# Feed-forward weights quantised inside the last two attention units, and a weight stage that only transposes

## The reference, cut to what matters

```python
h = _layernorm(x) * (1 + ca) + sa
x = x + ga * _L0_attn_ref(h, W_qkv, W_out)            # 16 heads, causal, ALiBi
h = _layernorm(x) * (1 + cb) + sb
x = x + gb * _L0_ffn_ref(h, w_gate, w_up, w_down)     # 704 x 256, 704 x 256, 256 x 704
...
def fp4_quant_dequant(x):        # along the last dim, blocks of 16
    scale = max(abs(xb)) / 6, at least 1e-12
    return nearest of (0, .5, 1, 1.5, 2, 3, 4, 6) to abs(xb / scale), * sign * scale
def _L0_ffn_ref(x, w_gate, w_up, w_down):
    gate, y = q(x) @ q(w_gate).T, q(x) @ q(w_up).T
    return q(silu(gate) * y) @ q(w_down).T
```

## Time and profile before

| | |
|---|---|
| median of 3 runs | 4037.24 us (4034.93 to 4038.52) |
| profiled execution | 4047.3 us, its span 4045.3 us |
| TensorE, VectorE, ScalarE, GpSimd busy over the span | 85%, 85%, 61%, 63% |
| attend's own work | 262 to 1245 us |
| last unit with row maxima | ends 1192 us |
| first instruction of prepare | 1249.56 us |
| first DMA of feed_forward | 1303.87 us |

### The profile page before, as it was taken

The page is one execution under the profiler, slowest core; times in us unless marked ns, Lnnn a source line. Parts: engine busy times, 40 slices in busy tenths (PEclk is TensorE's granted clock), DMA queues, the critical chain, the costliest instruction groups (busy, mean ns, idle before and its releaser), DMA issues. The chain is left out here.

```text
span 4045.3 us, 64173 instructions
## 1 busy us (share of the span) xinstructions
PE 3418.7 (85%) x22940; PEld 1634.9 (40%) x22940; DVE 3430.8 (85%) x5768; ACT 2465.4 (61%) x4542; POOL 2561.4 (63%) x2392
## 2 busy tenths in 40 slices
PE   5979999999994899999777888888888788777667
PEld 2633333333332555555433333333333333333366
DVE  5768888888863999999669999999999999999866
ACT  5626666666773344444477777777777777676422
POOL 1102232322331888888578999989989999888633
PEclk8979999999997999999898989888988999898689
DMA  4894656555532111111122332332233322322232
GB/s 137 282 198 64 88 72 90 78 82 83 82 47 73 38 49 45 46 45 40 34 75 61 88 89 80 83 83 74 76 82 86 86 78 77 87 71 72 57 101 82
DMA packets 291354, 329.66 MB, mean 81 GB/s; under 512 B 37375, under 2 KB 207478, under 8 KB 291030
## 3 DMA queue, kind: packets, MB, share of 16 engines
q1 hardware_dynamic: 291038, 325.58, 35.2%
HBM read 239.58 MB, written 85.03 MB: 80 GB/s over the span
## 5 line engine op out<-in xcount | busy, mean ns | idle before, releaser
L1898 POOL TENSOR_TENSOR d_dBu<-d_dtu,d_Bn 128x1024 f32<-128x1024 f32 x384 | 903.5, 2388 | 19.8 <-DVE d_dtu L2079 19.7
L752 ACT ACTIVATE b_P<-b_pT 128x512 f32<-128x512 f32 (+1 forms) x1120 | 571.7, 575 | 298.2 <-PE b_pT L658 295.2
L1678 ACT ACTIVATE d_dA<-d_dt,d_decay 128x512 f32<-128x512 f32 x768 | 524.4, 685 | 254.4 <-DVE d_h L2006 252.2
L785 DVE CUSTOM_DVE_ANT_0 b_pS<-b_pS,mask_qk 128x512 f32<-128x512 f32 (+1 forms) x768 | 501.7, 690 | 83.6 <-PE b_pS L668 74.2
L1886 POOL TENSOR_TENSOR d_h<-d_h,d_Cn 128x2048 f32<-128x2048 f32 x112 | 511.5, 4574 | 77.9 <-ACT d_last_h L1702 42.4
L630 POOL TENSOR_SCALAR_AFFINE_SELECT b_P<-b_P 128x128 f32<-128x128 f32 (+2 forms) x608 | 194.0, 323 | 513.6 <-ACT b_P L752 501.8
L2006 DVE TENSOR_TENSOR_SCAN d_h<-d_dA,d_last_h,d_dBu 128x512 f32<-128x512 f32 x384 | 462.1, 1263 | 47.3 <-PE d_y L1543 28.7
L668 PE MATMUL b_pS<-KS,QS 99*128 99x512 bf16 (+3 forms) x1536 | 475.1, 339 | 28.3 <-PEq L85 21.5
L2006 DVE TENSOR_TENSOR_SCAN d_h<-d_dA,d_dBu 128x512 f32<-128x512 f32 x384 | 443.2, 1207 | 52.8 <-PE d_y L1543 25.2
L658 PE MATMUL b_pT<-QS,KS 118*128 118x512 bf16 (+3 forms) x1536 | 449.3, 329 | 3.1 <-ACT b_P L752 2.1
L1543 PE MATMUL d_y<-d_h,d_eye 32*32 32x512 f32 x8192 | 345.4, 704 | 32.8 <-DVE d_h L2013 32.8
(11 more groups left out here) (352 smaller groups left out, 6735.3 us busy)
## 6 DMA issues: line engine op xcount, KB each, us to landing
d_Bn<-scratch_bs SPq DMA_DIRECT2D x128, 512.0 KB, 5.0
d_Cn<-scratch_bs SPq DMA_DIRECT2D x112, 256.0 KB, 3.4
scratch_parts<-a_part SPq DMA_DIRECT2D x48, 512.0 KB, 4.1
QS<-scratch_parts SPq DMA_DIRECT2D x192, 128.0 KB, 7.2
KS<-scratch_parts SPq DMA_DIRECT2D x192, 128.0 KB, 7.6
scratch_v<-a_v SPq DMA_DIRECT2D x16, 1024.0 KB, 7.6
V<-scratch_v SPq DMA_DIRECT2D x32, 512.0 KB, 11.6
a_x<-in_L_attn_x_dram SPq DMA_DIRECT2D x16, 512.0 KB, 7.7
```

Of the source, the lines that this page charges most:

```text
L752: act.activation(t[:, heads[0]:heads[-1] + 1, c * CH:c * CH + w], pT[:, place % RING, 0:len(heads) * w].rearrange("p (h w) -> p h w", w=w) ...
L785: last = dve.tensor_tensor_reduce(out=pS[:, j % RING, 0:w], in0=pS[:, j % RING, 0:w], in1=K["mask_qk"][:, 0:w], scale=-1.0, scalar=-MASKED ...
L1678: act.activation(to[:, m % 2, :], dt[:, c.k % 2, m, :], ACT.Exp, scale=decay[:, m, n:n + 1]).then_inc(dA_d, 1)
L1898: pool.tensor_tensor(product(c, n)[:, 2 * j:2 * j + 2, :], dtu[:, c.k % 2, 2 * j:2 * j + 2, :], Bn[:, n // BG % 2, n % BG, :].unsqueeze(1) ...
```

## The change

The tiles of the weights (`raw_gate`, `raw_up`, `raw_down`, `raw_wout`, and `raw_late`, which is the quantising scratch first and takes W_in, W_x and W_dt after it) are now allocated around `attend` and `prepare`, on the other side of SBUF. SyncE issues the five feed-forward loads and the eight of W_out in attention's step u = 8. VectorE clears the pad rows at attention's start, quantises gate and the first half of up after `normalise` of unit 29 (in unit 30's step), and the rest after `normalise` of unit 30 (in unit 31's step). SyncE then loads W_in, W_x and W_dt into the scratch, before the last store. `prepare` loads only base_W, the A and B matrices and a bias (11 DMAs and one), turns gate, up and down first, and copies every second piece out with VectorE.

```diff
+            def load_weights():
+                sp.wait_ge(pads, 2)
+                for w, name in ((gate, "L0_ffn_w_gate"), (up, "L0_ffn_w_up")):
+                    sp.dma_start(w[:, 0:KF - 1, :], A[name][0:(KF - 1) * P, :].rearrange("(r p) k -> p r k", p=P)).then_inc(ffn_in, 16)
+                    sp.dma_start(w[0:FR, KF - 1, :], A[name][(KF - 1) * P:FF, :]).then_inc(ffn_in, 16)
+                sp.dma_start(down[:, :, :], A["L0_ffn_w_down"].rearrange("(r p) k -> p r k", p=P)).then_inc(ffn_in, 16)
+                for r in range(KD):
+                    for i in range(NQB):
...
+            def load_late():
+
+                sp.wait_ge(q_done, 3)
...
             def step(m, u):
+                if u is not None and u.base * NG + u.k == 8:
+                    load_weights()
                 if m is not None and (not isinstance(m.base, int) or m.base * NG + m.k + 1 < total):
...
             units(sp, step)
+            load_late()
             store(LAST)
...
+            dve.memset(gate[FR:P, KF - 1, :], 0.0).then_inc(pads, 1)
+            dve.memset(up[FR:P, KF - 1, :], 0.0).then_inc(pads, 1)
...
+            def quantise_in_drain(u):
+
+                n = u.base * NG + u.k
+                if n == total - 2:
+                    dve.wait_ge(ffn_in, 16 * 5)
+                    block_scales(gate, KF * D)
+                    round_blocks(gate, KF * D)
+                    dve.wait_ge(q_done, 1)
+                    block_scales(up, KF * D)
+                if n == total - 1:
+                    round_blocks(up, KF * D)
+                    dve.wait_ge(q_done, 2)
+                    block_scales(down, KD * FF)
+                    round_blocks(down, KD * FF)
...
+                if u is not None:
+                    quantise_in_drain(u)
             units(dve, step)
...
         @block.tensor
         def _(pe):
-            pe.wait_ge(turn_in, 16 * (14 + KD * NQB))
             for j, (src, dst) in enumerate(turns):
-                if j == early:
-                    pe.wait_ge(q_done, 3)
+                if j == late:
+                    pe.wait_ge(late_in, 16 * (3 + KD * NQB))
+                if j == last:
+                    pe.wait_ge(turn_in, 16 * 11)
                 if j >= 8:
-                    pe.wait_ge(ev, j - 7)
+                    pe.wait_ge(ev if j % 2 == 0 else ev_dve, (j - 8) // 2 + 1)
...
         @block.vector
         def _(dve):
...
+            for j, (src, dst) in enumerate(turns):
+                if j % 2:
+                    dve.wait_ge(tr, j + 1)
+                    dve.tensor_copy(dst, turned(j)).then_inc(ev_dve, 1)
```

More of the change, by code:

```diff
@@ L476, in bank_pieces, with blocks, spread, late_weights @@
     return pieces
+DN, NS, DR, TAPS = 512, 16, 64, 4
+MD = DN // P
+QB = 32
+NQB = P // QB
+FB = 16
+FF = 704
+KF = -(-FF // P)
+FR = FF - (KF - 1) * P
+ROUND = 1.5 * 2.0 ** 22
+DOWN = 1.0 - 2.0 ** -23
+EXPONENT = 0x7F800000
+def blocks(t):
+    return t.rearrange("p (b e) -> p b e", e=FB)
+def spread(s, n):
+    return s.unsqueeze(2).to_broadcast([s.shape[0], n // FB, FB])
+def late_weights(late):
+    w_in = late[:, 0:8 * D].rearrange("p (r k) -> p r k", k=D)
+    w_x = late[0:DR + 2 * NS, 8 * D:8 * D + DN]
+    w_dt = late[:, 8 * D + DN:8 * D + DN + 4 * DR].rearrange("p (r k) -> p r k", k=DR)
+    return w_in, w_x, w_dt
 def attend(nc, A, S, K):
@@ L526, in attend @@
         sems += s_in + [alp_put]
+        ffn_in, late_in = S["ffn_in"], S["late_in"]
+        pads, q_step, q_done = sem("pads"), sem("q_step"), sem("q_done")
+        gate, up, down, late = K["raw_gate"], K["raw_up"], K["raw_down"], K["raw_late"]
+        W = KF * D
+        v, e = late[:, 0:W], late[:, W:2 * W]
+        amax, scale, inv = K["raw_amax"], K["raw_scale"], K["raw_inv"]
         s_mm, s_max, g_tr, g_ev, g_step, g_joined, gc_set, g_parts = (
@@ L834, in sem @@
             return sems[-1]
[L836 to L838 removed]
+        gate, up, down, w_out = K["raw_gate"], K["raw_up"], K["raw_down"], K["raw_wout"]
+        w_in, w_x, w_dt = late_weights(K["raw_late"])
+        base, acat = sb("base", [P, KD, D]), sb("acat", [118, D])
         bcat = sb("bcat", [P, KD, 7, 16])
[L840 to L842 removed]
         psT = [local.enter_context(nc.psum_tensor(f"w_psT{i}", [P, 512], F32)) for i in range(8)]
[L844 removed]
+        turn_in, tr, ev, ev_dve, bias_in = (sem(n) for n in ("turn_in", "tr", "ev", "ev_dve", "bias_in"))
+        late_in = S["late_in"]
+        sems += [S["ffn_in"], late_in]
         turns = []
+        for n, w in enumerate((gate, up)):
+            for r in range(KF):
+                rows = P if r < KF - 1 else FR
+                for k in range(KD):
+                    turns.append((w[0:rows, r, k * P:(k + 1) * P], K["guT"][:, k, n * FF + r * P:n * FF + r * P + rows]))
+        for r in range(KD):
+            for k in range(KF):
+                cols = P if k < KF - 1 else FR
+                turns.append((down[:, r, k * P:k * P + cols], K["downT"][0:cols, k, r * P:(r + 1) * P]))
+        late = len(turns)
         for r in range(8):
@@ L861, in prepare @@
                 turns.append((w_out[:, r, k * P:(k + 1) * P], K["w_outT"][:, k, r * P:(r + 1) * P]))
+        last = len(turns)
+        for r in range(KD):
             for k in range(KD):
@@ L867, in prepare, with turned @@
             turns.append((bcat[:, r, :, :].rearrange("p e r -> p (e r)"), K["bcatT"][0:112, r * P:(r + 1) * P]))
[L868 to L877, removed]
-        block = local.enter_context(nc.Block())
+        block = local.enter_context(nc.Block())
+        def turned(j):
+            src, dst = turns[j]
+            rows, cols = src.shape
+            t = psT[j % 8][0:cols, 0:rows]
+            return t.rearrange("p (i q) -> p i q", q=QB) if len(dst.shape) == 3 else t
         @block.sync
         def _(sp):
[L882 to L893, removed]
             sp.dma_start(base[:, :, :], A["L1_ffn_base_W"].rearrange("(r p) k -> p r k", p=P)).then_inc(turn_in, 16)
@@ L1269 @@
 NATURAL_SET = 6
-QB = 32
-NQB = P // QB
 PE_B = (5, 8, 11, 14)
@@ L2381, in build @@
             prepare(nc, A, S, K)
+            raw.close()
             feed_forward(nc, A, S, K)
```

85 lines of the change are left out of this document (36 added, 49 removed).

## The result

The changed kernel takes 4006.8 us (median of 4 runs, 4004.87 to 4008.9) against 4037.88 us for the kernel before on the same chip (4 runs): ratio 0.9924, 95% interval 0.9907 to 0.9941. The forecast was 4007.6. The profiled execution went from 4047.3 to 4008.9 us, its span from 4045.3 to 4006.8.

The account below looks back on a forecast made before the run. `prepare`, running alone between attention and feed-forward (load, VectorE's quantising, turns), was taken as the bound. 39.7 us gained less 10.0 of collision and 0.1 of clears gives 29.6: 4037.2 to 4007.6, forecast 4003 to 4012 (56%), range 3996 to 4018.

Parts of the forecast that it names:

- The load and the quantising leave `prepare`: At the seam, 9.7 us of load and 35.8 us of quantising go; feed_forward starts 39.7 us earlier.
- the term of the turns: In `prepare`, 76 turns in one row, 21 slow in 4.9 us and 55 in 8.0 us: together 13.3 us.
- The collision: In attention's last two units, GpSimd's selects and VectorE's blocking quantising instructions wait for each other: 10 us lost.
- The walk: Tile-by-tile estimate of select waits in units 30 and 31: 4.2 us and about 6 us.
- no collision: Rival for attention's last two units: selects and quantising run side by side, gain 38.6 us, time 3998.6; 23%.
- a heavy one: Rival: 16 selects in the last units each wait one mean blocking instruction, 18.4 us, time 4016.0; 15%.
- VectorE doesn't bound the drain: VectorE ends at about 1245, before unit 31's invert; the rival, VectorE bounding the drain and a slower kernel, had 2%.
- Late weights: In `prepare`, they land near 1252, before the 37th turn needs them; rival that turns wait, 4010 to 4020, 2%.
- SyncE's queue: Before unit 11's load, thirteen added DMAs take 12.5 us, covered by 21.3 us of idle queue: no cost.
- The sum: Whole kernel: 39.7 - 10.0 - 0.1 = 29.6 us less, profiled execution 4017.7, median 4007.6.

Follow-up runs that it names:

- Experiment 3: Changed kernel with the quantising back at the start of `prepare`, loads early and turns shared as in the change: 4030.3 us, ratio 0.9974.
- experiments 1: Changed kernel with VectorE's 30 quantising instructions left out, so weights stay unquantised: 3997.9 us, ratio 0.9894.
- 8: Changed kernel without quantising; VectorE does eight reductions in the step of attention's last unit instead: 4001.0 us, ratio 0.9897.
- 9: Changed kernel without quantising; VectorE does eight products of two SBUF tiles in the step of attention's last unit instead: 4008.1 us, ratio 0.9915.
- experiments 5: Changed kernel with the quantising's product scratch in PSUM and the late weights issued behind the last store: 4002.4 us, ratio 0.9901.
- 7: Changed kernel with scratch in PSUM, late weights behind the last store, and gate's first four quantising instructions moved before unit 29's invert: 4000.1 us, ratio 0.9894.
- experiment 2: Changed kernel with the quantising's product scratch in PSUM, late weights still before the last store: 4011.9 us, ratio 0.9922.
- 6: Changed kernel with each large quantising product and element-wise instruction cut into three of at most 512 columns: 4003.7 us, ratio 0.9903.
- 10: Changed kernel with the large quantising instructions cut in three and the late weights issued behind the last store: 4002.9 us, ratio 0.9902.
- experiment 4: Changed kernel with all 76 turned pieces copied out by ScalarE alone: 4010.0 us, ratio 0.9923.

## Why the prediction was right

**The load and the quantising leave `prepare`.** Forecast: 39.7 us from `prepare`, feed_forward's first DMA at 1264.2 if attention ended as before. Measured: the stretch from the first instruction of `prepare` to that DMA went from 54.3 us to 11.96 (1257.99 to 1269.95), 42.3 us less. The mechanism is as forecast; the term of the turns was too large, 13.3 us for what took 10.9 (1258.04 to the last copy's end, 1268.9). Most of it is the price of a turn at the fast clock, forecast at 0.145 us "between 0.09 and 0.17": some 17 turns lie in the slow 3.9 us (forecast 21 in 4.9), and the other 59 end at 1268.58, so 6.7 / 59 = 0.113 us each. Over all runs the slow part was 3.6 to 9.0 us, and from first turn to c_wo it took 11.8 to 14.3 us with the copies shared (forecast 14.4): this trace is at the short end. Experiment 3 divides the gain.

**The collision.** Forecast 10 us, 4.2 in unit 30 and about 6 in unit 31; measured 3.1 and 5.4, 8.5 in sum. (The walk's own parts for unit 31 are 4.0, 1.5 and 1, which make 6.5, and 10.7 in all.) The walk said which tiles: 1 (+2.0, measured 1.29), 2 (+1.5, 1.12) and 4 (+0.7, 0.71) in unit 30, and tile 1 of unit 31 as the worst (+4.0, measured 3.00). Tiles 2 and 3 of unit 31, forecast at 2.5 us together, cost about 0.4. What brought the unit near its forecast all the same is a part that the walk didn't contain: TensorE's clock fell to 0.50 during the wait, which cost some 2.0 us. So for unit 31 the mechanism was right and the size was in part luck. That no collision or a heavy one would come instead is excluded by the selects (5.57 us for four) and by experiments 1, 8 and 9. The walk also counted the element-wise and the small instructions as blocking. For the element-wise ones the change's own trace shows it, in the step of unit 31:

```profile
1237.69 0.89 DVE L860 TENSOR_SCALAR raw_late<-raw_late 128x1408 f32<-128x1408 f32 x1
```

```profile
1238.15 0.70 POOL L689 TENSOR_SCALAR_AFFINE_SELECT b_P<-b_P 128x256 f32<-128x256 f32 x1 [1.24 <-ACT b_P L811]
```

The select takes 0.70 us and not 0.41, and ends 0.27 us after the end of L860 (1238.58). The small ones are at least held up themselves: 0.30 us beside selects in unit 30 (L851 and L853 on up), 0.21 alone. That a select waits for a small one is not shown.

The rule of the Trainium skill (SBUF — State Buffer, Who interferes with whom) says this of products and reductions: products of two SBUF inputs block a GpSimd that reads SBUF, reductions don't. Experiments 8 and 9 agree with it, 22.53 against 28.61 us for one unit.

**VectorE doesn't bound the drain.** It was done at 1244.00, forecast about 1245, and 7.80 us before the last inversion. **Late weights.** Issued from 1244.03 on, 8.9 us ahead of the store as forecast (9), and TensorE shows no wait for them. **SyncE's queue.** Forecast 12.5 us for the thirteen DMAs under 21.3 us of idle queue. It was 17.8 us:

```profile
523.94 0.58 SPq L633 DMA_DIRECT2D raw_gate<-in_L_ffn_w_gate_dram  x1
524.56 3.88 SPq L634 DMA_DIRECT2D raw_gate<-in_L_ffn_w_gate_dram  x1
...
529.50 1.52 SPq L634 DMA_DIRECT2D raw_up<-in_L_ffn_w_up_dram  x1
...
531.71 10.04 SPq L639 DMA_DIRECT2D raw_wout<-in_L_attn_W_out_dram  x8
544.99 0.34 SPq L240 DMA_DIRECT2D QS<-scratch_parts  x1
```

The queue held the second DMA of gate for 3.88 us, where 0.55 was put in. The load of unit 11 still starts at 544.99, as before at 545.32. The cover that was left is 3.2 us.

**The sum.** 33.9 us at the seam against 29.6 forecast, and 31.1 in the medians. Both large terms were off the same way, the turns by 2.4 us and the collision by 1.5. So that the median came within 0.8 us of the forecast is luck: its interval (0.9907 to 0.9941) is 24 to 38 us of gain and holds 29.6 as well as 33.9. The profiled execution, forecast at 4017.7, took 4008.9. The spans of the two profiles differ by 38.5 us, which is 33.9 and 4.6 behind the seam. That second part can't be put down to the change: in the twelve profiles of changed kernels what comes behind c_wo's load is 2730 to 2741 us long (span less that start), though none of them differs from the others there. Its cause stays open. This spread of 10 us is larger than the 7 us by which experiments 5 and 7 improve the seam, so their times alone don't prove them faster than the change.

## What to carry to other kernels

Idle time of an engine in the drain of a stage is good cover, but ask which of the engines that still work share something with it: VectorE's reductions cost GpSimd nothing here, while products on SBUF stretched a group of four selects from 2.5 to 6.9 us, and taking their scratch to PSUM won back 6.8 of 8.5 us. What a wait of TensorE costs can be the wait and the slow matmuls behind it, here 3.0 and 2.0 us. And where a stage ends in a store and a barrier, look at what stands in front of the store, however early it seems: with the late weights 8.9 us ahead it cost nothing that shows, but as soon as they came closer it took 1.5 us (experiment 2 against 5) and 4.3 us (6 against 10).

## What the runs showed that I had not expected

How long TensorE stays at 1.2 GHz after the barrier doesn't follow from how long it stood in these runs. In the changed kernel it stood 6.27 us and was slow for 3.9 us of turns; with the eight reductions it stood 6.29 us and was slow for 8.9; with three pieces it stood 11.71 us and was slow for 4.6. Windows of the run with the reductions, the first 8.54 us of its turns:

```profile
1248.46:1257.00 8.54, 8.54 (x39) 7.58 (x40) 5.06 (x18) 4.92 (x19) 0.00 (x0) 0.50 0.28 58
```

This moved the turns by 2.5 us from kernel to kernel, about as much as sharing the copies is worth, and no run here explains it. When it falls in a wait isn't settled either: with 3.00 us of waiting the clock fell inside the wait in the changed kernel (at about 1231.2) and not at all behind the same wait in experiment 4, and with the eight products it fell at about 1232.1, 0.6 us after a wait of 4.35 us had ended. The other surprise is the DMA of 64 pad rows, 3.88 us of SyncE's queue for gate and 1.52 for the same shape of up, where 0.55 was put in. The queue's idle stretch covered it.
